# The first expert layer's matmuls, 128 columns wide, given as pairs of 64 columns on the two column halves of the TensorE array

## The reference

```python
# x is now x + first branch; t: tokens (N = 4096, D = 64), E = 8 experts, hidden 256
xn = (t - mean) * rsqrt(var + eps)                       # after one more LayerNorm
logits = xt @ Wr + br ; top-2 of softmax(logits), weights normalized to 1
xe = xn[None] * ln_g[:, None] + ln_b[:, None]
h = gelu(einsum('end,edh->enh', xe, W1) + b1)            # first layer: 64 -> 256
y = einsum('enh,ehd->end', h, W2) + b2                   # second layer: 256 -> 64
out = t + sum over the two chosen experts of weight * y
```

## Time and profile before

| | |
|---|---|
| median of 3 executions | 269.35 us (268.19 to 271.62) |
| profiled execution | 269.56 us |
| its span | 267.5 us, mean granted TensorE clock 0.942 |
| TensorE matmul busy | 231.0 us, 86% of the span, 1206 records |
| ScalarE busy | 129.5 us, 48% |
| VectorE busy | 149.3 us, 56% |
| GpSimd busy | 45.1 us, 17% |

### The profile page before, as it was taken

One profiled execution on the slowest core, in us unless ns is written; L12 is line 12 of the kernel. 1 busy time (PEld: TensorE's weight loads), 2 busy tenths in 40 slices (PEclk: granted clock), 3 DMA queues, 4 the chain that ended last, 5 costly groups with the idle time before them and its releaser, 6 DMA issues.

```text
span 267.5 us, 3160 instructions
## 1 busy us (share of the span) xinstructions
PE 231.0 (86%) x1206; PEld 121.8 (46%) x1206; DVE 149.3 (56%) x266; ACT 129.5 (48%) x206; POOL 45.1 (17%) x44
## 2 busy tenths in 40 slices
PE   3487689999985698969439999999999999999994
PEld 3385479757442477759324223222223333333331
DVE  0691939999696990676887324432443334433344
ACT  2147641021720707043637567556655676666760
POOL 3750077003770008202120000000000000000000
PEclk9869999999997959997957999999999999999999
DMA  7990000000000000000005907043150705043001
GB/s 235 209 208 8 2 0 4 0 0 2 0 0 0 1 0 2 0 0 0 2 1 143 192 1 157 0 108 91 49 108 2 194 2 142 16 104 96 0 0 39
DMA packets 6430, 14.18 MB, mean 53 GB/s; under 512 B 2704, under 2 KB 4112, under 8 KB 5392
## 3 DMA queue, kind: packets, MB, share of 16 engines
q1 hardware_dynamic: 6416, 13.99, 22.3%
HBM read 12.81 MB, written 1.18 MB: 52 GB/s over the span
## 4 chain that ended last, share of the span: by engine, by line
PE 72%; DVE 13%; ACT 8%; DMA 3%; issue 1%; SPq 1%; DVEq 0%; ACTq 0%
PE psum L611 22%; PE psum L626 22%; DMA xs<-in_x 3%; PE psum L524 3%; PE psum L470 3%; PE psum L442 3%; PE psum L452 3%; PE psum L540 2%; PE psum L478 2%; PE psum L487 2%; ACT place L661 2%; PE psum L383 1%; PE psum L558 1%; ACT place L722 1%; DVE place L957 1%; PE psum L433 1%
## 5 line engine op out<-in xcount | busy, mean ns | idle before, releaser
L768 ACT ACTIVATE hid<-psum,b1p 128x512 f32<-128x512 f32 x128 | 77.7, 688 | 41.3 <-PE psum L611 41.3
L611 PE MATMUL psum<-tok,w1s 128*128 128x512 f16 x256 | 64.4, 388 | 0.1
L1061 DVE SCALAR_TENSOR_TENSOR term<-psum,sm,wide 128x512 f32<-128x512 f32 x32 | 24.0, 751 | 70.8 <-PE psum L626 68.0
L626 PE MATMUL psum<-hid,w 128*64 128x512 f32 x256 | 61.8, 604 | 0.0
L611 PEld LDWEIGHTS psum<-tok,w1s 128*128 128x128 f16 x256 | 21.7, 99 | 51.3 <-ACT hid L768 28.0
L626 PEld LDWEIGHTS psum<-hid,w 128*64 128x64 f32 x256 | 15.6, 136 | 32.1 <-issue 26.3
L1066 DVE TENSOR_TENSOR x<-x,term 128x512 f32<-128x512 f32 x32 | 22.1, 692 | 1.1
L470 PE MATMUL psum<-h_pad,tap_bd 128*128 128x512 f32 x36 | 15.8, 592 | 0.0
L383 PE MATMUL psum<-c,xs 128*128 128x128 f32 x32 | 7.3, 423 | 8.3 <-DMA xs<-in_x 8.3
L895 DVE SCALAR_TENSOR_TENSOR place<-h_pad,sm,place 128x512 f32<-128x512 f32 x16 | 12.0, 752 | 0.6
L524 PE MATMUL psum<-place,wide 128*128 128x64 f32 x64 | 9.8, 327 | 2.7 <-DVE wide L964 2.7
(11 more groups left out here) (135 smaller groups left out, 306.0 us busy)
## 6 DMA issues: line engine op xcount, KB each, us to landing
wide<-gate_store SPq DMA_DIRECT2D x16, 512.0 KB, 6.4
xs<-in_x SPq DMA_DIRECT2D x2, 512.0 KB, 6.3
w1f<-in_W SPq DMA_DIRECT2D x2, 512.0 KB, 12.7
block_out<-x SPq DMA_DIRECT2D x4, 256.0 KB, 6.4
hid<-in_W1T SPq DMA_DIRECT2D x1, 512.0 KB, 12.2
w<-in_W SPq DMA_DIRECT2D x1, 512.0 KB, 14.8
c<-const SPq DMA_DIRECT2D x1, 483.5 KB, 4.0
sm<-in_small SPq DMA_DIRECT2D x1, 407.0 KB, 6.3
```

Of the source, the lines that this page charges most:

```text
L611: mm = pe.matmul(h_bank(n), w1s[:, part, e, k * P:(k + 1) * P], tok[:, pair, half, b, :], start=part == 0, stop=part == 1)
L626: mm = pe.matmul(y_bank(u)[b * H:(b + 1) * H, :], w2[:, e * KT + k, :], hid[:, u % 2, B2 * k + b, :], start=k == 0, stop=k == KT - 1)
L768: act.activation(hid[:, u % 2, t, :], h_bank(n), ACT.Gelu, bias=b1p[:, e * KT + k:e * KT + k + 1]).then_inc(gelu_ready, 1)
L1061: dve.scalar_tensor_tensor(term[:, u % 2, :], y_bank(u), b2t[:, e:e + 1], gate_b[part][:, e % (E // 2), :], ALU.add, ALU.mult).then_inc(te ...
```

## The change

In `up`, each matmul of 128 weight columns is given as two of 64 columns. The first takes columns 0 to 63 of the tile's weights and writes partitions 0 to 63 of the bank, the second columns 64 to 127 and partitions 64 to 127. Both stream the same 128x512 tokens. The semaphore is raised by the last of a tile's four matmuls. Nothing else is touched: 256 L611 matmuls with their 256 weight loads become 512 with 512, and the result is the same.

```diff
@@ -608,8 +608,10 @@
                     if before >= 0:
                         pe.wait_ge(gelu_ready, before + 1)
                     for part in range(2):
-                        mm = pe.matmul(h_bank(n), w1s[:, part, e, k * P:(k + 1) * P], tok[:, pair, half, b, :],
-                                       start=part == 0, stop=part == 1)
+                        for side in range(2):
+                            mm = pe.matmul(h_bank(n)[side * H:(side + 1) * H, :],
+                                           w1s[:, part, e, k * P + side * H:k * P + (side + 1) * H], tok[:, pair, half, b, :],
+                                           start=part == 0, stop=part == 1)
                     mm.then_inc(w1_done, 1)
 
             def down(u):
```

## The result

The changed kernel takes 261.26 us (median of 4, 261.01 to 262.45) against 269.0 us (median of 4) for the kernel before, run beside it: ratio 0.973, 95% interval 0.968 to 0.978. That is faster by 2.2% to 3.2%. The forecast was 262.6 us, with a range from 260.8 to 268.0. The profiled execution took 261.04 us, with a span of 259.0 us.

A forecast was written before the change was run, and what follows sets the result against it. TensorE's stream was taken to bound the expert phase. Gains of 4.0 (late), 2.7 (early) and 0.05 us (end) sum to 6.8, giving 262.8 for the profiled execution and a forecast of 262.6 us, range 260.8 to 268.0.

The forecast's parts named there:

- What bounds: Expert phase: TensorE is busy throughout, so whatever comes off its stream comes off the end time, until ScalarE is met.
- Drains by shape: At the two line changes of a unit: each change of array shape costs 0.09 or 0.10 us, plus unhidden loads.
- the gap belongs to the change of format: Rival at the line changes: 16-bit to 32-bit drains as before, no change that can be told, 271.1 us; chance 0.07.
- Late half: The 16 late expert units: both drains and unhidden loads go, 3.70 becomes 3.45 us a unit, 4.0 us in all.
- Early half: The 13 early expert units: one wait stays, 3.85 becomes 3.64 us a unit, 2.7 us in all.
- The wait itself: Early units: tile 3 still waits for the GELU of tile 0, its load starting 1.44 us after the block.
- Added instructions at zero: First-layer expert matmuls: 256 more matmuls and 256 more loads hide in the 0.216 us steps and cost zero.
- a lag that adds up: Rival: each pair's lag of 6 to 8 ns lengthens every L611 step, 264 to 268 us; chance 0.10.
- loads that are not hidden: Rival: 64-column 16-bit loads show 0.05 us in each step, half at 274 us and half above; chance 0.08.
- Halves one behind the other: Rival: the two matmuls of a first-layer pair run in turn, 47 us more, 316 us; chance 0.05.
- Edges: Around the expert phase: gains before 150.66 us hide behind the gates from DRAM; 0.05 us gained after the last L611 block.
- The 0.05 at the end: Two L626 blocks after the last L611 block: their first step loses 0.05 us.

The follow-up runs named there:

- e9: The changed kernel run again without an edit; median 262.84 us, ratio 0.977 to the kernel before.
- e1: Changed kernel with tiles 0 and 3 of each unit as 64-column pairs, tiles 1 and 2 as single 128-column matmuls; 267.27 us, ratio 0.992 to the kernel before.
- e2: Changed kernel with each tile's high part as a 64-column pair and its correction part as one 128-column matmul, eight shape changes a unit; 288.97 us, one run.
- e3: Changed kernel with the first layer as four matmuls of 32 columns, the second layer still on halves; 269.81 us, ratio 1.003 to the kernel before.
- e4: Changed kernel with both layers on four column quarters of 32; 263.09 us, ratio 0.978 to the kernel before.
- e6: Changed kernel with five banks for tiles and two for results from unit 3 on instead of unit 16; 258.74 us, ratio 0.960 to the kernel before.
- e8: Changed kernel with matmuls in groups of two tiles, four on the left half, then four on the right; 281.94 us, ratio 1.050 to the kernel before.

## Why the prediction was right

**What bounds.** TensorE's stream of experts has no idle time in either kernel, and what came off it came off the end: 7.2 us in the two stretches. The ratio's interval, 0.968 to 0.978 of 269.0, is 6.0 to 8.5 us, and e9's ratio of 0.977 lies within it.

**Drains by shape.** Right, and shown in three ways: moved inside a block between equal formats (e1), multiplied (e2: eight cost 0.94 us a unit, where the two of before cost 0.26, each time with the loads behind them), and brought back with another width and taken away again with equal widths (e3, e4). The rival that the gap belongs to the change of format fell with e1.

**Late half.** Forecast 3.45 us a unit and 4.0 us in all; measured 3.444 and 16 x 0.256 = 4.1.

**Early half.** Forecast 3.64 and 2.7; measured 3.613 and 13 x 0.238 = 3.1. This is the term that was mis-sized, by 0.4 us, of which 13 x 0.026 = 0.3 is one step and the rest rounding. The step at fault is "after a wait the first 64-column load is not hidden, 0.05 as at the first L626 pair": that row is of a 32-bit load. The 16-bit one shows half as much. Timeline of the changed kernel at tile 3 of an early unit:

```profile
152.55 0.62 PE L612 MATMUL psum<-tok,w1s 128*64 128x512 f16 x4
```

Four matmuls last 0.62 us together where four with their loads ahead last 0.60 (the rows at 202.60 and 202.82 above), so 0.024 and not 0.05. The load records fit: a 16-bit load takes 97 ns for 32 columns (e4) and 110 for 64, a 32-bit one 110 and 137. That is 13 and 27 ns for 32 columns, and by it, as an estimate, 26 and 54 ns for the 64 columns that must be loaded when nothing was loaded ahead. The wait itself was right: tile 3's load, which waits for tile 0's GELU, starts at 152.54, 1.43 after the block's start at 151.11 (forecast 1.44), and e6 removed it for 2.2 us.

**Added instructions at zero.** Right, and with room: e4 shows zero for four times the matmuls and loads of the first layer. The rivals of a lag that adds up and of loads that are not hidden fell with the step of 0.216: the second of a pair trails by 3 or 4 ns in the changed kernel, and the lag does not add up.

**Halves one behind the other.** Did not occur, as L626 had shown in 32-bit.

**Edges.** What was gained ahead of the second L628 block was hidden by the gates, as forecast: from the first expert matmul to that block are 9.40 us before and 9.48 after. The 0.05 at the end came too (the last 16 L626 records take 3.65 us, those of L628 3.60). In all, 6.8 us were forecast and 7.2 measured in the stretches; the 8.5 between the two spans includes 1.35 of drift. The medians scatter around that with their fronts: they fell by 7.7 us, and by 6.7 in e9 (269.54 to 262.84). Of the 1.3 us by which the forecast missed the median, 0.4 is the early half, 0.1 the late one and 0.35 the kernel before, which had 269.0 where 269.35 was assumed; what is left is front.

## What to carry to other kernels

Two kinds of matmul that alternate should use the array in one shape: here each change between matmuls of 128 and of 64 columns cost 0.11 to 0.13 us with the load behind it (e1, e2, before), one between 64 and 32 columns 0.13 (e3), and splitting the wide one cost nothing in the stream. The gap shows in no busy time; it is found by comparing the distances between starts at a change of line with those inside a block. And where a gain is a few per cent, compare the stretch that was changed: here its length repeated to 0.01 us while the total moved by 3.5 us with the same kernel.

## What was not expected of the hardware

- A matmul for one half of the array passes those that stand before it and wait for the other half, past three of them in e8, and starts 40 ns after its neighbour. The Trainium skill, TensorE: Matmul & The Clock Gate, Part 3 (packing small matmuls), says that matmuls start and end in the program's order; e8's block of 1.73 us instead of 2.6 is against that for the start. For completion e8 agrees with it: the semaphore comes 0.42 us after its own matmul and 0.03 after the last of those that stand before it.
- A 16-bit load of 64 columns that is not hidden lengthens the stream by 0.024 us, a 32-bit one by 0.051. The same page (LDWEIGHTS) gives columns / 1.2 ns, an estimate of 53 ns for both; what the 32-bit one adds agrees, what the 16-bit one adds does not, and the load records themselves are longer than either (137 and 110 ns).
- Between 16-bit and 32-bit matmuls of one shape no gap is seen in either direction: steps of 0.22 and 0.43 us at the line changes of the changed kernel, as inside its blocks.
